# Eight pipeline lags and DMA-turned f16 parts of x and y in a cross-attention and gene-gating kernel

## The reference

```python
# attention: x (16,128,512), ctx (16,128,256)
q = layernorm(x) @ Wq ; k, v = split(ctx @ Wkv)
q, k = rope(q, pos), rope(k, pos)
w = softmax(q k^T / 4)                    # per head, 128 x 128
x = x + (w v) @ Wout + bout
# gating
y = layernorm(x)
xn = y * rsqrt(mean(y*y) + eps) * norm_w
logits = xn @ Wc.T / clip(temperature, 0.1)       # 1024 genes
top_vals, top_idx = top_k(logits, 32)
expressed = softmax(top_vals) @ genes[top_idx]    # 64 columns
out = x + tanh(expressed @ Wd.T) * xn * (expressed @ Wu.T) * scale
```

## Time and profile before

| | us |
|---|---|
| three runs | 526.91, 529.2, 530.35 |
| median | 529.2 |
| span of the profiled execution | 527.0 |
| PE busy | 457.6 (87%) |
| DVE busy | 416.1 (79%) |
| POOL busy | 262.2 (50%) |
| ACT busy | 258.1 (49%) |

### The profile page before, as it was taken

One profiled execution on the slowest core, in us unless ns is written; L12 is line 12 of the kernel. 1 busy time (PEld: TensorE's weight loads), 2 busy tenths in 40 slices (PEclk: granted clock), 3 DMA queues, 4 the chain that ended last, 5 costly groups with the idle time before them and its releaser, 6 DMA issues. The chain is left out here.

```text
span 527.0 us, 10932 instructions
## 1 busy us (share of the span) xinstructions
PE 457.6 (87%) x3866; PEld 336.8 (64%) x3866; DVE 416.1 (79%) x644; ACT 258.1 (49%) x386; POOL 262.2 (50%) x263
## 2 busy tenths in 40 slices
PE   1727698999999999999999999999999999796734
PEld 0525465677776767676777777777677776565523
DVE  3574274989898989899998989898989897866680
ACT  2641626374737374645555463647464737243111
POOL 0453527282919292928374655647382919110111
PEclk9967699999999999999999999999999999979776
DMA  7940504141322314050505050505041321200000
GB/s 266 283 90 18 95 1 89 25 87 26 69 64 51 84 30 103 21 109 21 109 21 109 21 109 21 109 9 113 9 92 38 73 59 37 65 23 1 21 20 21
DMA packets 81754, 34.45 MB, mean 65 GB/s; under 512 B 73136, under 2 KB 75200, under 8 KB 81728
## 3 DMA queue, kind: packets, MB, share of 16 engines
q1 hardware_dynamic: 80768, 33.05, 27.1%
q10 hardware_dynamic: 960, 1.05, 0.6%
HBM read 12.86 MB, written 4.19 MB: 32 GB/s over the span
## 5 line engine op out<-in xcount | busy, mean ns | idle before, releaser
L830 DVE MAX8 top<-stage_b 128x8 f32<-128x1024 f32 x64 | 78.0, 1218 | 32.3 <-ACT stage_b L579 32.1
L396 POOL TENSOR_TENSOR rstd<-var,minus_half 128x1 f32<-128x1 f32 x16 | 8.8, 550 | 178.1 <-DVE var L804 178.1
L838 DVE MATCH_REPLACE8 stage_b<-top,stage_b 128x1024 f32<-128x1024 f32 x64 | 77.3, 1208 | 0.0
L367 POOL TENSOR_TENSOR stage_b<-stage_b,cos_t 128x512 f32<-128x512 f32 x32 | 41.2, 1288 | 37.0 <-issue 25.5
L994 PE MATMUL gene<-wcT_h,yT_h 128*128 128x512 f32 x128 | 53.9, 421 | 1.1 <-DVE yT_l L817 1.1
L994 PE MATMUL gene<-wcT_l,yT_h 128*128 128x512 f32 x128 | 51.8, 405 | 0.0
L994 PE MATMUL gene<-wcT_h,yT_l 128*128 128x512 f32 x128 | 51.6, 403 | 0.0
L1101 PE MATMUL dense<-stage_a,v_ext 128*32 128x128 f32 x1024 | 42.6, 287 | 2.8 <-ACT stage_a L552 2.1
L536 ACT ACTIVATE parts<-turned 128x1024 f16<-128x1024 f32 x32 | 33.8, 1057 | 19.1 <-POOL turned L380 19.1
L765 DVE TENSOR_REDUCE row_max<-score_a 128x8 f32<-128x1024 f32 x32 | 38.9, 1217 | 4.8 <-PE score_a L1060 4.8
L765 DVE TENSOR_REDUCE row_max<-score_b 128x8 f32<-128x1024 f32 x32 | 38.9, 1215 | 3.7 <-PE score_b L1060 3.5
(11 more groups left out here) (149 smaller groups left out, 1129.2 us busy)
## 6 DMA issues: line engine op xcount, KB each, us to landing
x_ring<-x_dram SPq DMA_DIRECT2D x16, 256.0 KB, 2.6
out_dram<-x_ring SPq DMA_DIRECT2D x16, 256.0 KB, 2.5
ctx_sb<-ctx_dram SPq DMA_DIRECT2D x16, 128.0 KB, 2.5
stage_a<-L_ffn_Wc_dram SPq DMA_DIRECT2D x1, 2048.0 KB, 10.1
stage_b<-L_xattn_Wq_dram ACTq DMA_DIRECT2D x1, 1024.0 KB, 5.9
stage_b<-L_xattn_Wkv_dram SPq DMA_DIRECT2D x1, 1024.0 KB, 9.3
stage_b<-L_xattn_Wout_dram SPq DMA_DIRECT2D x1, 1024.0 KB, 12.5
genes_sb<-L_ffn_genes_dram SPq DMA_DIRECT2D x2, 256.0 KB, 5.2
```

What stands on the lines that cost most here:

```text
L367: pool.tensor_tensor(halves(qk_cos), halves(qk_sb), trig(cos_t, t), ALU.mult).then_inc(s_cosm[n], 1)
L830: nc.vector.max(top[:, 8 * n:8 * n + 8], logit if n == 0 else rest).then_inc(s_top[n], 1)
L838: nc.vector.match_replace(rest, top[:, 8 * n:8 * n + 8], logit if n == 0 else rest, REMOVED).then_inc(s_rem[n], 1)
```

## The change

- x and y are turned by DMA. ACT and DVE or POOL split xn and yn in SBUF into two f16 parts (`x_hl`, `y_hl`, 128 by 2 by 512), and SP turns both parts in one transposing DMA each (`turn_x`, `turn_y`). `transpose_x`, `transpose_y` and the splits from PSUM are gone. Attention and context are turned on PE as before.
- Wq and Wc parts are f16, scaled by a power of two that is found on the chip: the largest magnitude per row (DVE), spread over all rows by a matmul (`spread`), its exponent (`power_of_two`). x and y carry a factor of 2048. `read_q`, `gene_exp` and `negate_top` undo it.
- Both norms are applied by ACT (`norm1_apply`, `norm2_apply`, as x times rstd plus shift); DVE computes the 128x1 shifts (`norm1_shift`, `norm2_shift`). yn goes into a ring of four, so the copy `keep` is gone. `x_lo` runs on POOL.
- Eight lags instead of six, an x ring of eight, and another order of the calls on every engine. On PE, ACT, DVE and POOL a tile's compute starts at t2.
- In SP's program the turn of tile 0's x stands ahead of the loads of Wc, bout, Wout, Wd, Wu and genes.

```diff
-XSLOTS = 6
+XSLOTS = 8
+YSLOTS = 4
-        wq_h, wq_l = sb("wq_h", [P, XK, DIM], f32r), sb("wq_l", [P, XK, DIM], f32r)
+        wq_h, wq_l = sb("wq_h", [P, XK, DIM], f16), sb("wq_l", [P, XK, DIM], f16)
-        wcT_h, wcT_l = sb("wcT_h", [P, XK, GENES], f32r), sb("wcT_l", [P, XK, GENES], f32r)
+        wcT_h, wcT_l = sb("wcT_h", [P, XK, GENES], f16), sb("wcT_l", [P, XK, GENES], f16)
...
 # SP
+            def turn_x(t):
...
+                sp.wait_ge(s_x_h, ready)
+                sp.wait_ge(s_x_l, ready)
+                if not first(t):
+                    sp.wait_ge(s_q, t)
+                sp.dma_start_transpose(xT[:].rearrange("p (m t) -> p m t", t=P),
+                                       x_hl[:].rearrange("p l d -> p (l d)")).then_inc(s_xT, 16)
...
+            def iteration(t0, t1, t2, t3, t4, t5, t6, t7):
+                    turn(t3, 0); next_x(t0); turn_x(t2); store(t7); shift(t3, 0); shift(t3, 1)
+                    next_ctx(t1); turn_y(t4); turn(t2, 1)
+            turn_x(0)
             sp.dma_start(wc_raw, wc.rearrange("(g p) d -> p g d", p=P)).then_inc(s_wc, 16)
...
 # POOL
+            def x_lo(t):
...
+                pool.tensor_tensor(x_hl[:, 1], xn[:], x_hl[:, 0], ALU.subtract).then_inc(s_x_l, 1)
...
+            def iteration(t0, t1, t2, t3, t4, t5, t6, t7):
+                    ln2(t5); rope(t3, 1); rope_sum(t3, 1); rope(t3, 0); rope_sum(t3, 0); split_lo(t3, 1)
+                    add_bout(t3); gate(t7); split_lo(t3, 0); ln1(t2); x_lo(t2); finish(t7)
...
 # ACT
+            def norm2_apply(t):
...
+                nc.scalar.activation(yn_of(t), slot(t), ACT.Identity, bias=shift2[:], scale=rstd2[:]).then_inc(s_yn, 1)
...
+            def iteration(t0, t1, t2, t3, t4, t5, t6, t7):
+                    read_wT(t7, 0); read_wT(t7, 1); neg_max_hi(t4); read_k(t3); norm2_apply(t5); y_hi(t5)
+                    read_q(t3); exp_group(t4, 0); exp_group(t4, 1); split_hi(t3, 1); e_hi(t7)
+                    exp_group(t4, 2); exp_group(t4, 3); read_oT(t4, 0); read_oT(t4, 1); tanh(t7)
+                    split_hi(t3, 0); attn_hi(t4); norm1_apply(t2); gene_exp(t6); read_v(t3); x_hi(t2)
+                    read_logits(t5, 0); read_logits(t5, 1); ctx_hi(t2)
...
 # DVE
+            def code_scale():
+                dve.wait_ge(s_small, 16 * 4)
+                find_largest(NORM, norm_sb[:])
+                dve.wait_ge(s_wc, 16)
+                find_largest(WC, stage_a[:])
+                power_of_two(NORM)
+                power_of_two(WC)
...
+            def iteration(t0, t1, t2, t3, t4, t5, t6, t7):
+                    attn_lo(t5); norm1_shift(t3); negate_top(t7); remove_top(t7, 3); mask(t7); residual(t5)
+                    group_max(t4, 0); group_max(t4, 1); group_max(t4, 2); ctx_lo(t3); group_max(t4, 3)
+                    norm2_stats(t5); neg_max_lo(t4); norm2_shift(t5); norm1_stats(t2)
+                    find_top(t6, 0); remove_top(t6, 0); find_top(t6, 1); y_lo(t5); e_lo(t7)
+                    remove_top(t6, 1); find_top(t6, 2); remove_top(t6, 2); normalise(t4); combine(t7)
+                    find_top(t6, 3)
...
 # PE
+            def iteration(t0, t1, t2, t3, t4, t5, t6, t7):
+                    transpose_max(t4); project_q(t3); scoresT(t4, 0); scoresT(t4, 1); express(t7)
+                    scoresT(t4, 2); values(t4, 0); scoresT(t4, 3); values(t4, 1); down_up(t7, 0)
+                    values(t4, 2); values(t4, 3); down_up(t7, 1); transpose_o(t4); logits(t5, 0)
+                    transpose_attn(t4); project_v(t3); project_out(t4); scores(t3, 0); scores(t3, 1)
+                    logits(t5, 1); scores(t3, 2); transpose_ctx(t2); transpose_w(t6, 0); scores(t3, 3)
+                    transpose_w(t6, 1); project_k(t2)
```

More of the change, by code:

```diff
@@ L39 @@
 REMOVED = -3.0e38
+NORM_UNIT = 2.0 ** 11
+WEIGHT_UNIT = 2.0 ** 13
+EXPONENT = 0x7F800000
+SMALLEST = 2.0 ** -100
+WQ, WC, NORM = range(3)
 ROPE_FREQS = [10000.0 ** (-j / 4) for j in range(4)]
@@ L243, in run @@
             with eng.Fori(lags + 1, TILES) as i:
+                for n in range(1, lags):
+                    eng.to_reg(i - n)
                 iteration(*(i - n if n else i for n in range(lags)))
@@ new lines, in turn_y @@
+            def turn_y(t):
+                ready = t + 1
+                hold(sp)
+                sp.wait_ge(s_y_h, ready)
+                sp.wait_ge(s_y_l, ready)
+                if not first(t):
+                    sp.wait_ge(s_lg[0], t)
+                    sp.wait_ge(s_lg[1], t)
+                sp.dma_start_transpose(yT[:].rearrange("p (m t) -> p m t", t=P),
+                                       y_hl[:].rearrange("p l d -> p (l d)")).then_inc(s_yT, 16)
+            def iteration(t0, t1, t2, t3, t4, t5, t6, t7):
+                if t3 is not None:
+                    turn(t3, 0)
@@ L320, in iteration @@
                 if later(t0, 1):
                     next_x(t0)
-                if t2 is not None:
-                    shift(t2, 1)
-                if t1 is not None:
-                    turn(t1, 0)
-                    turn(t1, 1)
-                if t5 is not None:
-                    store(t5)
-                if later(t0):
-                    next_ctx(t0)
-                if t1 is not None:
-                    shift(t1, 0)
-            run(sp, 6, iteration)
+                if later(t2):
+                    turn_x(t2)
@@ new lines, in iteration @@
+                if t7 is not None:
+                    store(t7)
+                if t3 is not None:
+                    shift(t3, 0)
+                    shift(t3, 1)
+                if later(t1):
+                    next_ctx(t1)
+                if t4 is not None:
+                    turn_y(t4)
+                if t2 is not None:
+                    turn(t2, 1)
+            turn_x(0)
+            sp.dma_start(wc_raw, wc.rearrange("(g p) d -> p g d", p=P)).then_inc(s_wc, 16)
+            sp.dma_start(bout_sb[:], bout.rearrange("(o n) -> o n", o=1).broadcast_to([P, DIM])).then_inc(s_small, 16)
@@ L335, in _ @@
+            run(sp, 8, iteration)
             sp.wait_ge(s_out, TILES * 16)
@@ L450, in _ @@
             add_bout(0)
-            run(pool, 6, iteration)
+            run(pool, 8, iteration)
         @block.scalar
@@ L959, in _ @@
+            run(dve, 8, iteration)
         @block.tensor
```

611 lines of the change are left out of this document (323 added, 288 removed).

## The result

| | before | after |
|---|---|---|
| median of 4 runs, us | 528.06 (526.04 to 530.35) | 522.64 (522.0 to 523.03) |
| span of the profiled execution | 527.0 | 520.6 |

The ratio is 0.989 (95% interval 0.986 to 0.992): 5.4 us less where 13.2 were forecast (516 against the median of 529.2 that the three runs listed above have; with the fourth run it is 528.06). The time lies in the forecast range of 500 to 530, but most of the gain is missing.

A forecast was written before the change was run, and what follows sets the result against it. PE was taken as the bound. Start 50.8, first periods 25, 23.5 and 26, twelve of 26.6 and drain 70 sum to 514.5, 12.5 under the span's 527.0; from the median of 529.2 the forecast was 516, range 500 to 530.

The forecast's parts named there:

- PE sets the pace: Full iteration before: PE, busy 27.12 of 27.6 us, is the bound, with DVE 2.3 us behind it.
- PE's own work, 25.5: PE per tile: 27.65 less 0.98 for transposes, 0.3 for f16 and 0.9 for edges and gaps gives 25.5 us.
- Period 26.6: Between starts of the maxima's transpose: PE's 25.5 plus 1.1 of waits, 1.05 under the 27.65 of before.
- The walk: One pass through the new loop from the maxima's transpose, working out which engine waits: 1.1 us of PE waits.
- POOL's chain: Rival, POOL's rope to split of q: with slow rope sums, scores come 1.6 us later per period, 537 us; chance 0.13.
- Waits of PE for the small DMAs: New loop: PE waits 0.5 us per period for the negated maximum's DMAs, with only the q projection as cover.
- First three periods, 74.5: After the first maxima's transpose: 25, 23.5 and 26 us, against 27.8, 25.9 and 27.7 before, partly filled.
- Start, 50.8: Up to the first maxima's transpose: 50.8 us against 49.45, with the Wc load behind tile 0's turn of x.
- Drain, 70: After the last maxima's transpose: 69.9 us instead of 64.3, with tile 15's mask at 54 and 15.8 after it.
- Gaps filled: Rival, PE in the loop: waits vanish because DMAs land sooner, period 25.5, 500 us; chance 0.20.
- Turned blocks one by one: Rival, turning DMAs: blocks are turned one after the other, small turns land after 10 us, 590 us; chance 0.02.
- late hand-overs: Rival, turned y, turned q and attention's low part: little slack, 0.9 us more per period, 528 us; chance 0.20.

The follow-up runs named there:

- e7: Kernel before with the 16 logits matmuls that have a low part left out (3.7 us less PE per tile): 528.9 us, 0.999.
- e17: Kernel before, 8 of 24 logits matmuls, high part of k later on ACT, root of the next norm earlier on POOL: 518.3 us, 0.978.
- e6: Changed kernel with the 16 logits matmuls that have a low part left out: 513.4 us, 0.971, loop period 25.90.
- e13: Changed kernel with POOL's bias sum moved behind the low part of q: 519.55 us, 0.982, loop period 25.60.
- e5: Changed kernel run again without any edit: 522.36 us, 0.986, loop period 26.03.
- e12: Changed kernel with 8 of 24 logits matmuls and three rounds of the top search instead of four: 509.2 us, 0.963.
- e2: Changed kernel with DVE's statistics of tile 1 moved ahead of the scale of Wc: 519.28 us, 0.984.
- e4: Changed kernel with DVE's low part of y placed ahead of the first search of the tile before: 534.7 us, 1.014.
- e3: Changed kernel with loads of Wc and bias ahead of tile 0's turn of x, and tile 1's statistics ahead of Wc's scale: 517.0 us, 0.979.
- e1: Changed kernel with the loads of Wc and the bias moved ahead of tile 0's turn of x on SP: 520.35 us, 0.986.
- e9: Changed kernel with eight idle f16 matmuls (1.72 us) added per tile on PE: 547.3 us, 1.035, period 27.33.
- e18: Kernel before, all matmuls, high part of k later on ACT, root of the next norm earlier on POOL: 540.3 us, 1.025.
- e10: Kernel before with 8 of 24 logits matmuls and three rounds of the top search instead of four: 527.0 us, 0.997.
- e11: Changed kernel with three rounds of the top search instead of four, 2.5 us less for DVE: 527.2 us, 0.998.

## Why the prediction was off

- **"PE sets the pace", before: fell.** The earlier trace rows show 27.12 busy of 27.6, and I took the busy share for the bound. e7 took 3.7 us away for nothing. The engines wait for each other in a cycle of nearly the same length (e17), which PE's work fills almost exactly.
- **PE's own work, 25.5: right in the main.** I took 2.2 us off the period of 27.65; PE's busy time fell by as much, from 27.12 to 24.95. The split was off: an f16 matmul takes 17 ns less in place of 8, 0.3 us per tile more over 36 of them, so turns and edges together gave less than I took. It mattered little in the loop, where e6 shows that PE's time is worth next to nothing below the cycle.
- **Period 26.6: 26.36, for another reason.** The walk had the low part of q done at 15.0 and its turn landed at 19.5 "just in time"; in the rows they are at 14.6 and 19.2 behind the transpose, just in time indeed. POOL's chain was walked rightly and filed as a rival for the case that it gets longer, but what stands behind it was the bound already (e13). What the walk missed is its other branch: the gate, DVE's `combine` and the low part of attention, for which PE waits 0.5 where 0.1 was forecast. Waits of PE for the small DMAs in the loop were at most 0.2, not 0.5.
- **First three periods, 74.5: 80.9. The step that failed most, by 6.4 us.** I took 2.8, 2.4 and 1.7 us off the three periods of before as "partly filled", where the steady gain was forecast as 1.05. The trace of before speaks against such a gain: its starts give 27.81, 26.36 and 27.47 (the prediction read the last two as 25.9 and 27.7), so with less work than a full period's 27.65 they are nearly as long, and the change shortened the three together by 0.7 and not 7. In the first one DVE has 9.5 us of work, but each hand-over of the newest tile is there: DVE sits idle for 11.0 us until the turned output, and PE, at a granted clock of 0.80 (0.82 before), needs more for the projections. An ACT table load of 1.28 us stands ahead of the first exponential. This chain of the newest tile is read from the rows; no run tried it alone. It is not q's turn as in the loop: here the scores start 5.3 to 7.0 us behind the issue of it.
- **The second and third period, not by the chain alone.** The kernel before has a granted clock of 1.00 in both. The changed kernel has 0.99 and 0.94 in one profile (25.44 and 27.54 us) and 0.93 and 0.88 in e5's (27.06 and 28.08). e6, with less work for PE, has 0.90 and 0.97 (25.60 and 24.19); e12, with still less, 0.99 and 0.87 (23.63 and 27.14). So PE's work and the clock count for some microseconds there, and how the missing 6.4 split between chain and clock stays open.
- **Start, 50.8: 53.5.** The load of Wc behind the turn of x was forecast (scales at 30.7, measured at 30.9; the largest took 4.41). Missed was what is queued behind it: the statistics of tile 1, so POOL's root, so rope of q (e2). Both repaired, the first maxima's transpose came some 7 us sooner than in e4 (e3).
- **Drain, 70: 69.8.** Right in the sum, in part by luck: the mask of tile 15 came 52.3 us behind the last transpose and not 54, and what follows took 17.5 and not 15.8; e5 has 68.0 for the same kernel. The turn of y lands after 3.1 us and not 4.4. The unrolled iterations, 0.6 us longer than the loop's, were not foreseen.
- **Rivals.** Gaps filled: no. Turned blocks one by one: no, eight land in 3.1 us, 16 in 4.3. Of "late hand-overs", one period had it, the loop's first: the scores started 6.0 us behind q's turn, and the period was 27.67. It is no accident: e1, e2, e3 and e5 have the same in the same iteration. POOL's chain: it does hold the period, as that rival said, but at 0.4 us and not at the 1.6 that I gave it.

Against the forecast of -12.5 in the span, measured -6.4: 6.4 from the first periods and 2.7 from the start are missing, 2.8 came back in the other twelve and 0.2 in the drain.

Open: whether PE's order alone holds e13 at 25.6 (PE is busy 24.95, waits 0.3 for the low part of the expressed row, and has small gaps), why q's turn lands late in the loop's first iteration, and how the steady gain of 1.6 us splits between f16, DMA turns and order. e9 says only that PE's saved time was needed: without 1.72 of it, 1.30 is lost.

## What to carry to other kernels

An engine that is busy 98% of a period need not be its bound: walk the whole cycle from one hand-over to its own next occurrence, over all engines and queues, and test it by taking work away. Look for what stands in an in-order queue in front of the step that the cycle passes; one such swap gave 0.4 us per tile of the loop here. Look at which engine really waits at the step: here two ways arrived within 0.03 us of each other, and only one of them showed as a wait. Moving a step later moves all behind it on its engine, and an order that helps with less work can hurt with more (e17, e18). Don't take a period to be shorter because it is partly filled: the three of the kernel before had 27.8, 26.4 and 27.5 against 27.65. And when work is taken away for a test, compare periods at the same granted clock: with less work on PE, e7 and e10 had 0.94 in iterations where the full kernel had 1.00.

## What the hardware showed

The two DVE operations shown here that read two tensors in SBUF and POOL's tensor operations shut each other out: the low part of y went from 0.68 to 1.79, a 128x1 shift from 0.16 to 1.23, and POOL's product from 1.28 to 1.73. The Trainium skill, "Advanced Engine Details and Errata", GPSIMD Details, says that POOL shares a read and a write interface with DVE and conflicts with DVE instructions that have two SBUF inputs; the rows agree, and add that the later one ends about as if it had waited for the earlier. Around 0.1 us in who starts first goes with a period of 26.83 or 26.03 (e11 and the changed kernel, which differ in DVE's work too).

At full clock an f16 matmul of 512 columns follows another after 216 ns, an f32r one after 233. A DMA turn of 8 blocks lands after 3.1 us (median), of 16 after 4.3, with one straggler of 6.0. The Trainium skill, "VectorE: DVE Perf Modes", The three transpose paths, gives 1309 ns for one block, by which eight would be an estimated 10.5 us; the measurement decides, they are not turned one after the other at that price.
